# A two-layer Mamba stack with a soft mixture of experts: the second output projection ahead of x_proj, silus one scan later, the next chunk's w sooner

## The chip, the cores and the metric

The kernel runs on one core of one Trainium2 chip. The metric is the device time of one execution in microseconds (us). Everything is float32. The engines are named as in the profile: PE (matmuls and transposes; PEld loads its weights), DVE (vector), ACT (activations and copies), POOL (GpSimd), SP (issues DMAs).

## The reference

The input is 8192 rows of 512 numbers. Two Mamba layers are followed by a soft mixture of experts. Nearly all the time goes to the Mamba layers, and the change touches nothing else. One layer computes

```python
xz = x @ W_in.T;  xc, z = split(xz)              # 1024 channels each
u = silu(causal_conv4(xc) + b_c)
dt, Bm, Cm = split(u @ W_x.T)                    # 32, 16, 16 columns
delta = softplus(dt @ W_dt.T + b_dt)
h[t] = exp(delta * A) * h[t-1] + delta * u * Bm  # 16 states per channel
y = ((h * Cm).sum(states) + u * D) * silu(z)
out = y @ W_out.T
```

## The kernel before, in words

**Chunks, scans, slots.** Each layer works in 16 chunks of 512 rows: 32 chunks, numbered 0 to 31, in one unbroken stream over both layers. A chunk has 128 slots; two slots make a *scan step*, so a chunk has scan steps 0 to 63. Four scan steps do one half of the pairs (16 states, 2 halves of the channels), two blocks of 128 channels at a time.

**What each engine does in scan step p.**

- POOL (`inputs`, L1172) makes `bu`, the product of `w = delta * u` and the row of B. `bu` has three buffers, so the one for scan p can start when scan p-3 has ended.
- ACT (`head` L938, `decay_of` L928) copies the first elements of `bu` and makes two `decay` tiles. These have four buffers, two per scan, so the decays for scan p can start when scan p-2 has ended. Then it does what the timetable gives to the two slots: it *takes* finished tiles of PE out of PSUM, scales every fourth turned state (`product`, L958), and runs the silus and the softplus.
- DVE (`scan`, L1289) runs the scan over `decay` and `bu` into `h`, and then the multiply-adds (`add_state`, L1319, L1317) of the two turned states of the two slots. Where ACT takes both of them, which is in every scan step p = 2 modulo 4, DVE has no multiply-add.
- PE turns the states (128x128 transposes, L666) into two PSUM banks (`turn`), which alternate; a bank is free again when DVE or ACT has used it. Between the turns it runs the projections of the timetable, a few matmuls a slot, into two other banks (`proj`, `RING = 2`). Projection tile n waits until tile n-2 has been taken by ACT.

**The order.** Every engine runs its own list in order. `ORDER` (L41) is the order of the projection tiles of a chunk; `timetable` (L112 on) spreads their matmuls over the slots by weights and sets the slot in which ACT takes each tile: three slots after its last matmul, changed by `TAKE_LATER`. `conv_half` and `conv` are the input projection and the convolution of the next chunk, `x_proj`, `turn_c`, `delta_next` its x_proj, the turned C and the first half of its delta; `delta` is the second half of the present chunk's; `out` 0 to 3 is the output projection of the chunk before; `gate` 0 to 7 is z; `norm` 0 to 3 (chunks 0 to 13 alone) transposes the normalised rows of the chunk two later.

**The silus.** `silu_u` (L829) runs once per half over a 128x2048 tile, `silu_z` (L871) likewise. Each lies between two loads of ACT's function table. `SILU_LATER` (L54) gives how many slots after the last take of its half each silu stands. The matmuls of x_proj need both `silu_u`; the earliest slot of x_proj is worked out from `SILU_LATER[1]` too (L126).

**The w of the next chunk.** Between its `bu`, POOL adds up the softplus (`sum_delta`, L1154) and multiplies by u (`product`, L1161), in the scan steps that `W_AT` (L58) gives; `HEAD_AT` (L61) places the small operations that make the first elements of the next chunk (L1181 to L1200). Two more of POOL's jobs, the sums of products (L1214, L1223), lie at fixed places (`SUM_AT`).

**x_proj out of PSUM.** ACT's take of x_proj (L837 to L843) copies the tile, issues two DMAs and only then frees the bank. `turn_c` needs the copied tile.

Of the kernel before, what the change touches and what calls it, by code (L numbers as in the profile page):

```python
# [40 lines left out]
ORDER = [('conv_half', 0, 0), ('conv_half', 1, 0), ('delta', 4, 0), ('conv', 0, 8), ('conv_half', 2, 0), ('delta',  # L41
         5, 0), ('conv', 1, 0), ('conv_half', 3, 0), ('delta', 6, 0), ('conv', 2, 0), ('delta', 7, 0), ('conv_half',
         4, 0), ('conv', 3, 0), ('conv_half', 5, 0), ('conv', 4, 0), ('conv_half', 6, 0), ('conv', 5, 0),
         ('conv_half', 7, 0), ('conv', 6, 0), ('conv', 7, 0), ('norm', 0, 0), ('out', 0, 0), ('norm', 1, 8), ('norm', 2, 0),
         ('x_proj', 0, 0), ('norm', 3, 0), ('turn_c', 0, 0), ('out', 1, 0), ('delta_next', 0, 0),
         ('delta_next', 1, 0), ('out', 2, 0), ('delta_next', 2, 0), ('delta_next', 3, 4), ('out', 3, 0), ('gate', 0,
         4), ('gate', 1, 0), ('gate', 2, 0), ('gate', 3, 0), ('gate', 4, 0), ('gate', 5, 0), ('gate', 6, 0),
         ('gate', 7, 0)]
# [1 line left out]
SLOTS_BODY = GROUPS * HB  # L50
PAIRS = SLOTS_BODY // 2
TAKE_LAG, TAPS_LEAD, XDBL_LAG, CONV_LAG, PROD_LAG = 3, 2, 3, 3, 2
TAKE_LATER = {('out', 0): -1, ('gate', 0): 1, ('gate', 2): 2, ('delta_next', 0): -1, ('conv', 5): -1, ('delta', 5): -1}
SILU_LATER = (4, 4, 1, 1)  # L54
V_SUM_AT = (10, 10, 10, 10, 10, 10, 10, 9, 9, 9, 10, 10, 10, 10, 10, 9)
JOIN_AT = (41, 72)

W_AT = {13: ('sum', 2), 16: ('product', 2), 20: ('sum', 3), 23: ('product', 3), 47: ('sum_next', 0), 51:  # L58
        ('product_next', 0), 55: ('sum_next', 1), 59: ('product_next', 1)}

HEAD_AT = {24: ('exponent', 1), 28: ('state', 1), 56: ('exponent_next', 0), 61: ('state_next', 0)}  # L61
HEAD_EXP_AT = {51: ('exp', 1), 117: ('exp_next', 0)}
BFIRST_AT = 24

# [51 lines left out]
def timetable():  # L116
# [5 lines left out]
    for i, (kind, x, earliest) in enumerate(ORDER):  # L122
        if kind == "conv":
            earliest = max(earliest, end_of["conv_half", x] + CONV_LAG + TAKE_LATER.get(("conv_half", x), 0))
        if kind == "x_proj":
            earliest = end_of["conv", NB - 1] + TAKE_LATER.get(("conv", NB - 1), 0) + TAKE_LAG + SILU_LATER[1] + 4  # L126
        if kind in ("turn_c", "delta_next"):
            earliest = end_of["x_proj", 0] + XDBL_LAG + TAKE_LATER.get(("x_proj", 0), 0)
        slots = []
# [9 lines left out]
        end = end_of[kind, x] = slots[-1]  # L139
        late = end + TAKE_LAG + TAKE_LATER.get((kind, x), 0)  # L140
        if kind == "conv_half":
# [5 lines left out]
        if kind == "conv" and x % HB == HB - 1:  # L147
            take[late + SILU_LATER[x // HB]].append(("silu_u", x // HB, i))
        if kind == "gate" and x % HB == HB - 1:
            take[late + SILU_LATER[2 + x // HB]].append(("silu_z", x // HB, i))  # L150
    return work, take, end_of
# [142 lines left out]
def mamba_stack(nc, ctx, d, rstd, nmr):  # L294
# [828 lines left out]
    def _(pool):  # L1123
# [17 lines left out]
        def bias(X):  # L1141

            pool.wait_ge(norm_step, X * 11 + 11)
            rows = slice(X * J, X * J + J)
            pool.tensor_tensor(nmr[:, rows], neg_mean[:], rstd[:, rows], ALU.mult).then_inc(bias_set, 1)
# [91 lines left out]
        def body(G, kind):  # L1237
            for p in range(PAIRS):
                what, pair = W_AT.get(p, ("", 0))
                if what and kind.has(what.replace("sum", "delta").replace("product", "delta")):  # L1240
                    delta_w(G, what, pair)
                if p == BIAS_AT and kind.norms:
                    bias(G + NORM_AHEAD)
                if p in HEAD_AT:
                    what, hf = HEAD_AT[p]
                    X = G + what.endswith("_next")
# [906 lines left out]
```

## Time and profile before

| | us |
|---|---|
| median of 3 runs (7781.32 to 7786.65) | 7782.45 |
| the profiled execution's own time | 7782.23 |
| its span (first to last instruction) | 7780.4 |
| chunks 2 to 30, first scan to first scan of the next | 221.2 to 224.0 each |
| stretch before the first scan | 99.2 |
| stretch behind the last scan (mixture of experts) | 580.6 |
| DVE busy, share of the span | 7073.6, 91% |
| PE busy, share of the span | 7040.2, 90% |
| POOL busy, share of the span | 6668.8, 86% |
| ACT busy, share of the span | 6030.5, 78% |

The page lists what each engine was busy with and what ended its idle time. The trace behind it gives each instruction with its start (from the span's start), its duration and, in square brackets, the idle time of its engine before it and what ended that. All chunks of one kind repeat to a tenth of a microsecond, so one chunk can stand for many: chunk 20 (4541.3 to 4763.1) for the chunks without `norm`, chunk 8 (1875.9 to 2098.4) for those with it.

### The profile page before, as it was taken

Reading aid. Unit: us, or ns where it says so; the run is one execution under the profiler, and the core shown is the slowest. Engines: PE = TensorE matmul, PEld = TensorE weight load, DVE = VectorE, ACT = ScalarE, POOL = GpSimd, SP = SyncE. Lnnn points to the kernel's source line nnn. Section 1 sums busy time; section 2 is a strip of 40 time slices with the busy share of each in tenths; the row PEclk is TensorE's granted clock in tenths of the full one; section 3 lists DMA queues with packets and bytes.
Section 4 is the critical chain, followed back from the end, with each engine's and each line's share of the span. In section 5 each row is a group of like instructions: output and inputs, shape, how many; then the busy total and the mean of one; then the engine's idle time right before and its main releaser. Section 6 shows DMA issues by size and latency. Waiting matters only on the chain. (4 is left out here: it accounts for less than half of the span.)

```text
span 7780.4 us, 98947 instructions
## 1 busy us (share of the span) xinstructions
PE 7040.2 (90%) x29580; PEld 3887.5 (50%) x29580; DVE 7073.6 (91%) x6228; ACT 6030.5 (78%) x13267; POOL 6668.8 (86%) x3115
## 2 busy tenths in 40 slices
PE   7899999999999999999999999999999999987799
PEld 3454554554454545544444445444444454444664
DVE  5999999999999999999999999999999999999655
ACT  7888888888878888877777788777777787776564
POOL 5999999999999999999999999999999999998010
PEclk9899999999999999999999999999999999998899
DMA  3222222222222222222222222222222222221665
GB/s 107 76 85 86 79 86 77 79 76 82 86 85 79 86 77 79 77 84 87 85 69 75 66 75 70 75 71 75 68 74 66 75 70 76 70 71 51 246 234 184
DMA packets 282695, 684.05 MB, mean 88 GB/s; under 512 B 37872, under 2 KB 38128, under 8 KB 254384
## 3 DMA queue, kind: packets, MB, share of 16 engines
q1 hardware_dynamic: 252464, 626.31, 24.7%
q10 hardware_dynamic: 29696, 51.40, 1.8%
q8 instruction: 239, 3.92, 0.2%
q14 instruction: 296, 2.42, 0.1%
HBM read 508.76 MB, written 168.82 MB: 87 GB/s over the span
## 5 line engine op out<-in xcount | busy, mean ns | idle before, releaser
L1172 POOL TENSOR_TENSOR bu<-w,b_rep 128x1022 f32<-128x1022 f32 x2048 | 4802.0, 2363 | 489.6 <-DVE h L1289 483.1
L1289 DVE TENSOR_TENSOR_SCAN h<-decay,bu 128x1024 f32<-128x1024 f32 x2048 | 4651.4, 2282 | 213.3 <-ACT decay L928 109.2
L666 PEld LDWEIGHTS turn<-ident_m,h 128*128 128x128 f32 x16384 | 1974.0, 143 | 2687.0 <-issue 1297.0
L928 ACT ACTIVATE decay<-delta,neg_a 128x511 f32<-128x511 f32 x4096 | 2666.4, 685 | 714.1 <-DVE h L1289 711.2
L666 PE MATMUL turn<-ident_m,h 128*128 128x128 f32 x16384 | 2573.5, 282 | 503.5 <-DVE acc L1319 465.6
L1319 DVE SCALAR_TENSOR_TENSOR acc<-turn,c_now,acc 128x512 f32<-128x512 f32 x2816 | 1972.6, 738 | 126.6 <-PE turn L666 126.2
L958 ACT ACTIVATE prod<-turn,c_now 128x512 f32<-128x512 f32 x1024 | 700.5, 684 | 504.2 <-PE turn L666 487.0
L1214 POOL TENSOR_TENSOR prod<-prod 128x1024 f32<-128x1024 f32 x448 | 1059.9, 2366 | 10.0 <-ACT prod L958 10.0
L588 PE MATMUL proj<-x_conv,w_in 128*128 128x512 f32 x2048 | 1026.2, 598 | 45.3 <-ACT halo L818 36.1
L588 PE MATMUL proj<-conv_in,conv_diag 128*128 128x512 f32 x1984 | 989.8, 598 | 68.3 <-ACT halo L818 68.3
L588 PE MATMUL proj<-x_gate,w_in 128*128 128x512 f32 x2048 | 1016.9, 596 | 0.0
L588 PE MATMUL proj<-zy,w_out 128*128 128x512 f32 x1024 | 504.5, 595 | 0.0
L588 PE MATMUL proj<-w_out,zy 128*128 128x512 f32 x1024 | 503.6, 598 | 0.9 <-DVE zy L1328 0.9
L938 ACT COPY bu<-h_first 128x2 f32<-128x2 f32 x2048 | 385.4, 188 | 51.5 <-ACT stage L877 25.5
L588 PEld LDWEIGHTS proj<-conv_in,conv_diag 128*128 128x128 f32 x1984 | 316.2, 191 | 212.3 <-ACT halo L818 108.4
L588 PEld LDWEIGHTS proj<-x_conv,w_in 128*128 128x128 f32 x2048 | 327.5, 192 | 184.0 <-issue 106.5
L588 PEld LDWEIGHTS proj<-x_gate,w_in 128*128 128x128 f32 x2048 | 327.9, 192 | 113.6 <-issue 107.4
L1154 POOL TENSOR_TENSOR delta<-delta,w 128x1024 f32<-128x1024 f32 x128 | 303.1, 2368 | 41.2 <-ACT w L862 41.2
L808 ACT ACTIVATE conv_diag<-ident_m,par 128x128 f32<-128x128 f32 x992 | 315.2, 391 | 0.4
L588 PE MATMUL proj<-u,w_x 128*64 128x512 f32 x512 | 305.6, 707 | 10.2 <-ACT u L829 10.2
L1161 POOL TENSOR_TENSOR w<-delta,u 128x1024 f32<-128x1024 f32 x128 | 303.7, 2373 | 0.3
L1317 DVE TENSOR_SCALAR acc<-turn,c_now 128x512 f32<-128x512 f32 x256 | 189.3, 741 | 106.1 <-PE turn L666 104.0
(167 smaller groups left out, 5839.9 us busy)
## 6 DMA issues: line engine op xcount, KB each, us to landing
b_rep<-b_rows SPq DMA_DIRECT2D x1024, 256.0 KB, 3.3
u_rows<-u SPq DMA_DIRECT2D x64, 1024.0 KB, 4.0
u_back<-u_rows SPq DMA_DIRECT2D x256, 256.0 KB, 3.5
x_gate<-xt SPq DMA_DIRECT2D x32, 1024.0 KB, 7.0
xt<-stage ACTq DMA_DIRECT2D x128, 256.0 KB, 2.4
x_conv<-xt SPq DMA_DIRECT2D x31, 1024.0 KB, 6.3
x_gate<-in_x_dram SPq DMA_DIRECT2D x16, 1024.0 KB, 5.3
x_l<-in_x_dram SPq DMA_DIRECT2D x16, 1024.0 KB, 10.3
```

What stands on the lines that cost most here:

```text
L588: mm = pe.matmul(out[0:lhs.shape[1], :], lhs, rhs, start=n == 0, stop=n == count - 1)
L666: mm = pe.transpose(out[:, b * P:(b + 1) * P], h[:, (G * GROUPS + k) % H_RING, b, j * P:(j + 1) * P], ident[:])
L808: act.activation(conv_diag[:, b % 2, k, :], ident[:], ACT.Copy, scale=par[:, STATES + k, b:b + 1])
L928: act.activation(decay[:, (G * SLOTS_BODY + s) % DEC_RING, 1:T], delta[:, blk, 1:T], ACT.Exp, scale=neg_a[:, n, blk:blk + 1]).then_inc(dec ...
L938: act.copy(bu[:, (G * PAIRS + p) % BU_RING, :, 0], h_first[:, hf, n, 2 * pr:2 * pr + 2]).then_inc(head_set, 1)
L958: act.activation(prod[:, V_BUFFER[q], k % 2, :], turn[:, BANK[tile], :], ACT.Copy, scale=c_now[:, j, n:n + 1]).then_inc(v_done, 1)
L1154: pool.tensor_tensor(delta[:, lo:lo + 2, :], delta[:, lo:lo + 2, :], w[:, lo:lo + 2, :], ALU.add).then_inc(delta_set, 1)
L1161: pool.tensor_tensor(w[:, lo:lo + 2, :], delta[:, lo:lo + 2, :], u[:, lo:lo + 2, :], ALU.mult).then_inc(w_set, 2)
L1172: pool.tensor_tensor(bu[:, (G * PAIRS + s // 2) % BU_RING, :, 1:T], w[:, blk:blk + 2, 1:T], b_rep[:, g % B_RING, 1:T].unsqueeze(1).to_broa ...
L1214: pool.tensor_tensor(total, total, prod[:, V_BUFFER[q]], ALU.add).then_inc(vsum_set, 1)
L1289: dve.tensor_tensor_scan(h[:, (G * GROUPS + k) % H_RING, 2 * pr:2 * pr + 2, :].rearrange("p b t -> p (b t)"), decay[:, at:at + 2, :].rearr ...
L1319: dve.scalar_tensor_tensor(out, src, scalar, out, ALU.mult, ALU.add).then_inc(x_done, 1)
```

## The change

Four tables are changed; no instruction is added or removed, and DVE's order stays as it is.

```diff
-         ('conv_half', 7, 0), ('conv', 6, 0), ('conv', 7, 0), ('norm', 0, 0), ('out', 0, 0), ('norm', 1, 8), ('norm', 2, 0),
-         ('x_proj', 0, 0), ('norm', 3, 0), ('turn_c', 0, 0), ('out', 1, 0), ('delta_next', 0, 0),
+         ('conv_half', 7, 0), ('conv', 6, 0), ('conv', 7, 0), ('norm', 0, 0), ('out', 0, 0), ('norm', 1, 8),
+         ('out', 1, 0), ('x_proj', 0, 0), ('norm', 2, 0), ('norm', 3, 0), ('turn_c', 0, 0), ('delta_next', 0, 0),
...
-TAKE_LATER = {('out', 0): -1, ('gate', 0): 1, ('gate', 2): 2, ('delta_next', 0): -1, ('conv', 5): -1, ('delta', 5): -1}
-SILU_LATER = (4, 4, 1, 1)
+TAKE_LATER = {('out', 0): -1, ('gate', 0): 1, ('gate', 2): 2, ('turn_c', 0): -1, ('conv', 5): -1, ('delta', 5): -1}
+SILU_LATER = (6, 6, 4, 4)
...
-W_AT = {13: ('sum', 2), 16: ('product', 2), 20: ('sum', 3), 23: ('product', 3), 47: ('sum_next', 0), 51:
-        ('product_next', 0), 55: ('sum_next', 1), 59: ('product_next', 1)}
-
-HEAD_AT = {24: ('exponent', 1), 28: ('state', 1), 56: ('exponent_next', 0), 61: ('state_next', 0)}
+W_AT = {13: ('sum', 2), 16: ('product', 2), 20: ('sum', 3), 23: ('product', 3), 46: ('sum_next', 0), 49:
+        ('product_next', 0), 52: ('sum_next', 1), 56: ('product_next', 1)}
+
+HEAD_AT = {24: ('exponent', 1), 28: ('state', 1), 54: ('exponent_next', 0), 60: ('state_next', 0)}
```

What the timetable makes of it, in scan steps of a chunk:

| | before | changed |
|---|---|---|
| `silu_u` first half (ACT) | 20 | 21 |
| take of `out` 0 (ACT) | 32 | 32 |
| `silu_u` second half (ACT) | 32 | 33 |
| `out` 1 matmuls (PE) | 38 to 40 | 32 to 35 |
| x_proj matmuls (PE) | 34 to 36 | 35 to 38 |
| `norm` 2 and 3 transposes (PE) | 32 and 37 | 38 and 38 |
| take of x_proj (ACT) | 38 | 40 |
| `turn_c`, `delta_next` 0 and 1 (PE) | 38, 41, 41 | 40, 40, 40 |
| `silu_z` first half (ACT) | 56 | 57 |
| `silu_z` second half (ACT) | 1 of the next chunk | the same |
| last `gate` take (ACT) | 0 of the next chunk | 63 |

**ACT, chunks without `norm`, around the second half of `silu_u`** (scan steps 31 to 34). `decay` are the tiles for the scan, `stage` is the take of `out` 0, `prod` scaled turned states. Before:

```order
L958 ACTIVATE prod<-turn,c_now 128x512 x2
L938 COPY bu<-h_first 128x2
L928 ACTIVATE decay<-delta,neg_a 128x511 x2
L969 COPY h_last<-h 128x4
L829 ACT_TABLE_LOAD
L829 ACTIVATE u<-u 128x2048
L772 ACT_TABLE_LOAD
L877 COPY stage<-proj 128x512
L879 DMA xt<-stage 128x512
L938 COPY bu<-h_first 128x2
L928 ACTIVATE decay<-delta,neg_a 128x511 x2
```

Now:

```order
L958 ACTIVATE prod<-turn,c_now 128x512 x2
L938 COPY bu<-h_first 128x2
L928 ACTIVATE decay<-delta,neg_a 128x511 x2
L969 COPY h_last<-h 128x4
L877 COPY stage<-proj 128x512
L879 DMA xt<-stage 128x512
L938 COPY bu<-h_first 128x2
L928 ACTIVATE decay<-delta,neg_a 128x511 x2
L829 ACT_TABLE_LOAD
L829 ACTIVATE u<-u 128x2048
L772 ACT_TABLE_LOAD
L938 COPY bu<-h_first 128x2
```

The silu with its two loads has moved behind the decays of scan 33, and the take of `out` 0 stands ahead of those decays.

**PE, chunks with `norm`, the middle of the chunk** (scan steps 32 to 38). `u,w_x` is x_proj, `zy,w_out` is `out`, `ident_m,x_gate` is `norm`, `ident_m,h` the turned states. Before:

```order
L588 MATMUL proj<-zy,w_out 128x512 x2
L666 MATMUL turn<-ident_m,h 128x128 x4
L694 MATMUL proj<-ident_m,x_gate 128x128 x8
L666 MATMUL turn<-ident_m,h 128x128 x16
L588 MATMUL proj<-u,w_x 64x512 x2
L666 MATMUL turn<-ident_m,h 128x128 x4
L588 MATMUL proj<-u,w_x 64x512
```

Now, first ahead of x_proj and then behind its last matmul:

```order
L588 MATMUL proj<-zy,w_out 128x512 x2
L666 MATMUL turn<-ident_m,h 128x128 x4
L694 MATMUL proj<-ident_m,x_gate 128x128 x4
L588 MATMUL proj<-zy,w_out 128x512
L666 MATMUL turn<-ident_m,h 128x128 x4
L588 MATMUL proj<-zy,w_out 128x512
L666 MATMUL turn<-ident_m,h 128x128 x4
```

```order
L588 MATMUL proj<-u,w_x 64x512
L694 MATMUL proj<-ident_m,x_gate 128x128 x8
L666 MATMUL turn<-ident_m,h 128x128 x12
L634 MATMUL proj<-ident_m,xdbl 128x128 x4
L641 MATMUL proj<-xdbl,w_dt 128x512
L666 MATMUL turn<-ident_m,h 128x128 x4
L641 MATMUL proj<-xdbl,w_dt 128x512
```

The run of turned states without a projection between them (x16 before) is filled with `out` 1, and `norm` 2 and 3 stand together right behind x_proj. In chunks without `norm` the rows are the same without the L694 ones.

**POOL, the last third of a chunk** (scan steps 46 to 59). `delta` and `w` are the sums and products of the next chunk. Before:

```order
L1154 TENSOR_TENSOR delta<-delta,w 128x1024
L1172 TENSOR_TENSOR bu<-w,b_rep 128x2x511 x4
L1214 TENSOR_TENSOR prod<-prod 128x1024
L1161 TENSOR_TENSOR w<-delta,u 128x1024
L1172 TENSOR_TENSOR bu<-w,b_rep 128x2x511 x4
L1214 TENSOR_TENSOR prod<-prod 128x1024
L1154 TENSOR_TENSOR delta<-delta,w 128x1024
L1172 TENSOR_TENSOR bu<-w,b_rep 128x2x511
L1181 TENSOR_TENSOR a_first<-neg_a,delta 128x64
L1172 TENSOR_TENSOR bu<-w,b_rep 128x2x511 x3
L1214 TENSOR_TENSOR prod<-prod 128x1024
L1161 TENSOR_TENSOR w<-delta,u 128x1024
```

Now:

```order
L1154 TENSOR_TENSOR delta<-delta,w 128x1024
L1172 TENSOR_TENSOR bu<-w,b_rep 128x2x511 x3
L1161 TENSOR_TENSOR w<-delta,u 128x1024
L1172 TENSOR_TENSOR bu<-w,b_rep 128x2x511 x2
L1214 TENSOR_TENSOR prod<-prod 128x1024
L1172 TENSOR_TENSOR bu<-w,b_rep 128x2x511
L1154 TENSOR_TENSOR delta<-delta,w 128x1024
L1172 TENSOR_TENSOR bu<-w,b_rep 128x2x511 x2
L1181 TENSOR_TENSOR a_first<-neg_a,delta 128x64
L1172 TENSOR_TENSOR bu<-w,b_rep 128x2x511
L1214 TENSOR_TENSOR prod<-prod 128x1024
L1172 TENSOR_TENSOR bu<-w,b_rep 128x2x511
```

The same operations stand between the same `bu`, the last product (L1161) now three `bu` sooner.

## Rows read from the trace of the kernel before

**Rows 1.** The page, part 1: busy time (share of the span) and instructions of each engine.
```profile
PE 7040.2 (90%) x29580; PEld 3887.5 (50%) x29580; DVE 7073.6 (91%) x6228; ACT 6030.5 (78%) x13267; POOL 6668.8 (86%) x3115
```

**Rows 2.** Busy time by stretch: stretch, length, busy of PE, PEld, DVE, ACT, POOL, clock.
```profile
4541.00:4763.00 222.00, 203.74 (x856) 109.83 (x855) 209.54 (x169) 174.64 (x384) 207.01 (x97) 0.98 0.22 72
4657.00:4662.00 5.00, 3.90 (x8) 1.47 (x8) 5.00 (x5) 1.99 (x3) 3.38 (x2) 0.50 0.16 35
```

**Rows 3.** Timeline of DVE, chunk 20: start, us, what, [idle before, releaser].
```profile
4609.46 2.28 DVE L1289 TENSOR_TENSOR_SCAN h<-decay,bu 128x1024 f32<-128x1024 f32 x1
...
4614.24 2.29 DVE L1289 TENSOR_TENSOR_SCAN h<-decay,bu 128x1024 f32<-128x1024 f32 x1 [1.19 <-ACT decay L928]
...
4649.36 2.29 DVE L1289 TENSOR_TENSOR_SCAN h<-decay,bu 128x1024 f32<-128x1024 f32 x1
...
4655.11 2.29 DVE L1289 TENSOR_TENSOR_SCAN h<-decay,bu 128x1024 f32<-128x1024 f32 x1 [2.15 <-ACT decay L928]
...
4665.46 0.75 DVE L1317 TENSOR_SCALAR acc<-turn,c_now 128x512 f32<-128x512 f32 x1 [2.38 <-PE turn L666]
...
4667.72 2.28 DVE L1289 TENSOR_TENSOR_SCAN h<-decay,bu 128x1024 f32<-128x1024 f32 x1
...
4671.08 0.75 DVE L1317 TENSOR_SCALAR acc<-turn,c_now 128x512 f32<-128x512 f32 x1 [0.44 <-PE turn L666]
...
4680.61 0.75 DVE L1319 SCALAR_TENSOR_TENSOR acc<-turn,c_now,acc 128x512 f32<-128x512 f32 x1 [0.26 <-PE turn L666]
...
4730.26 2.29 DVE L1289 TENSOR_TENSOR_SCAN h<-decay,bu 128x1024 f32<-128x1024 f32 x1 [1.09 <-POOL bu L1172]
...
4738.29 2.29 DVE L1289 TENSOR_TENSOR_SCAN h<-decay,bu 128x1024 f32<-128x1024 f32 x1 [0.94 <-ACT decay L928]
```

**Rows 4.** Timeline of ACT, chunk 20, at the two `silu_u`.
```profile
4607.47 1.28 ACT L829 ACT_TABLE_LOAD   x1
4608.76 1.91 ACT L829 ACTIVATE u<-u 128x2048 f32<-128x2048 f32 x1
4610.69 1.28 ACT L772 ACT_TABLE_LOAD   x1
...
4652.65 0.59 ACT L877 COPY stage<-proj 128x512 f32<-128x512 f32 x1
...
4653.63 0.19 ACT L938 COPY bu<-h_first 128x2 f32<-128x2 f32 x1 [0.40 <-ACT stage L877]
4653.73 1.29 ACT L928 ACTIVATE decay<-delta,neg_a 128x511 f32<-128x511 f32 x2
```

**Rows 5.** Timeline of PE, chunk 20, scan steps 32 to 36.
```profile
4648.42 1.88 PE L588 MATMUL proj<-w_out,zy 128*128 128x512 f32 x4
...
4658.10 1.11 PE L666 MATMUL turn<-ident_m,h 128*128 128x128 f32 x4 [4.43 <-DVE acc L1319]
4659.14 3.68 PE L588 MATMUL proj<-u,w_x 128*64 128x512 f32 x4
```

**Rows 6.** Timeline of POOL, chunk 20, from the `bu` of scan 45 on.
```profile
4690.64 2.36 POOL L1172 TENSOR_TENSOR bu<-w,b_rep 128x1022 f32<-128x1022 f32 x1 [1.08 <-DVE h L1289]
...
4741.86 4.72 POOL L1172 TENSOR_TENSOR bu<-w,b_rep 128x1022 f32<-128x1022 f32 x2
```

**Rows 7.** Timeline of PE, chunk 8, end of `out` 0 and `norm` 1.
```profile
1984.86 1.88 PE L588 MATMUL proj<-zy,w_out 128*128 128x512 f32 x4
...
1987.02 0.60 PE L694 MATMUL proj<-ident_m,x_gate 128*128 128x128 f32 x4
```

**Rows 8.** Timeline of ACT, chunk 8, the take of x_proj.
```profile
2007.47 0.58 ACT L837 COPY xdbl<-proj 64x512 f32<-64x512 f32 x1 [0.63 <-PE proj L588]
...
2008.91 0.16 ACT L843 COPY spare_m<-proj 128x1 f32<-128x1 f32 x1 [0.87 <-ACT xdbl L837]
```

**Rows 9.** Timeline of DVE, chunk 8: scans 32 and 36.
```profile
1985.73 2.28 DVE L1289 TENSOR_TENSOR_SCAN h<-decay,bu 128x1024 f32<-128x1024 f32 x1
...
2003.10 2.28 DVE L1289 TENSOR_TENSOR_SCAN h<-decay,bu 128x1024 f32<-128x1024 f32 x1
```

## The prediction

> **What bounds the kernel now.** I read the page first: DVE and PE are busy 91% and 90% of the span, POOL 86% [rows 1]. Over one chunk DVE works 209.5 of 222 us, POOL 207.0, PE 203.7 [rows 2]. So no engine can save more than its idle 12.5 us in a chunk, and since DVE's own list is unchanged, the question is where those 12.5 us lie. DVE's timeline says it [rows 3]: it never drifts, it stops at a few fixed places. In chunk 20 these are scan 21 (1.19 us, waits for the decay), scan 33 (2.15, the decay), the multiply-adds behind scan 35 (2.38, waits for PE), those behind 36 and 39 (0.44, 0.26), scan 55 (1.09, waits for POOL) and scan 57 (0.94, the decay). The chain of waits on the page covers only the tail and tells nothing of this. About 0.2% of 7782, or 16 us, is what a measurement here can tell from no change.
>
> The pace between stops, from the same timeline: a scan takes 2.2 us of DVE's time and two multiply-adds 1.3, so a step is 3.5 us, or 2.2 where ACT takes both states (p = 2 modulo 4).
>
> **Silus, the rule.** A silu holds ACT for 1.28 + 1.91 + 1.28, 4.50 us with the hand-overs [rows 4]. The decays for scan p may start at the end of scan p-2 and take 1.39 us with the head copy (4653.63 to 4655.02 [rows 4]). With the silu behind them, the next decays end 1.39 + 4.50 + 1.39 = 7.3 us after that start, plus ACT's other work; DVE needs them three sets of multiply-adds and two scans later: 8.3 us if all three have two, 7.0 if one is empty. Steps 20, 32 and 56 have an empty one; 21, 33 and 57 do not. This is what the move buys.
>
> **Scan 21.** The take of `conv_half` 5 (three copies, 4611.97 on) now goes ahead of them, in free time. The decays of 21 start at the end of scan 19 (4609.46 less 1.3 of multiply-adds, 4608.2) and end at 4609.65, the silu ends at 4614.2, the take of `conv` 4 (0.7) at 4614.9, the decays of 22 at 4616.25. Scan 22 is due at 4609.46 + 7.0 = 4616.46 [rows 3]. The 1.19 go. But ACT's scaled states two steps on come late against the faster DVE, and PE may not turn the second state of step 23 before its bank is free; following that chain (turn 0.45, matmul 0.87, turn, matmul, turn) gives back 0.7. **Gain 0.5 per chunk**; bounds 0 and 1.2. All 31 chunks.
>
> **Scans 33 to 39 without `norm`** (chunks 14 to 30, 17 of them). ACT now takes `out` 0 ahead of the decays of 33. PE ends `out` 0 at 4650.30 [rows 5], so ACT, done with the decays of 32 by then, waits; its copy and DMA issue cost 0.98 (4652.65 to 4653.63 [rows 4]); the decays of 33 end at 4652.7, just in time for 4649.36 + 3.5 = 4652.86 [rows 3]. The silu ends at 4657.3, the decays of 34 at 4658.75, but scan 34 is due at 4656.36: a stop of 2.5, one scan later than the old 2.15. So the silu itself gains nothing here. What goes is what came behind it. Before, PE has nothing but turns between `out` 0 and x_proj, stands 4.43 us, and then runs the first two x_proj matmuls in 3.68 us [rows 5]. The granted clock there is 0.50, the lower level of 1.2 GHz [rows 2]; at 2.4 GHz they would need half. That is why the adds behind 35 wait 2.38. Now `out` 1 fills the hole: PE turns and multiplies in pairs of 1.3 us, two pairs a step against 3.5, and stands at most 1.4 us. Scan 34 starts at 4658.85, 35 at 4661.05, 36 at 4664.55, where the trace has 4667.72 [rows 3]: 3.2 us. The x_proj pairs (1.6 us each, 3.2 per step) fit under DVE's 3.5, so 0.44 and 0.26 go too. **Gain 3.9**; bounds 0 (the clock falls all the same) and 5.
>
> **The same place with `norm`** (chunks 0 to 13, 14 of them). `out` 0 ends at 1986.74 and `norm` 1 stands between [rows 7]; `out` 1's first matmul delays the next turn to 1988.9 where the add is due at 1988.58 (1985.73 + 2.85 [rows 9]): 0.35. The decays of 33 end at 1989.2, the silu at 1993.8, the take of `norm` 1 (0.98) at 1994.8, the decays of 34 at 1996.2, scan 36 starts at 2002.0 against 2003.10 [rows 9]: 1.1 better. Then the two PSUM banks bite. `norm` 3 stands on PE two tiles behind x_proj and waits until ACT has freed x_proj's bank; ACT takes x_proj only behind the decays of 40, after scan 38 (2011.2), and frees the bank 1.6 us after it begins (2007.47 to 2009.07, with two DMA issues [rows 8]): at 2015.0. All turns queue behind `norm` 3 on PE, so the add behind scan 39, due at 2013.4, gets its state at 2016.1: a stop of 2.7. **Loss 0.7 by scan 40** in place of a gain; bounds a gain of 2.5 (no such stop) and a loss of 3.
>
> **x_proj, turn_c, delta_next (scans 40, 41).** PE: turned C at 136.0 us of the chunk, `delta_next` 0 to 137.4, `delta_next` 1 when ACT has taken the turned C (137.6, behind the decays of 41), `out` 2 when ACT has taken `delta_next` 0 (138.7), the next turned state at 140.2, needed at 141.7. 1.5 to spare: nothing. SP's queue keeps its order; b_rows is stored two scan steps later, and its reader is the next chunk's.
>
> **The w of the next chunk.** From scan 45 on POOL does not wait for anyone until the `bu` of 59: it starts at 4690.64 and starts that one at 4741.86 [rows 6]. In between lie the same operations as before, so its end cannot move. Before, w is last of them and the stops are at 51, 55 and, hidden under POOL, at 57. Now POOL's work comes at 52 and 56, so DVE meets it at 51, 52, 55 and 56; by 2.3 us per POOL operation the `bu` of 56 is ready at 4735.1, and 3.5 + 3.5 + 2.8 later scan 59 starts at 4745.0, 0.4 after today's. The 0.94 at scan 57 vanish under it. **Loss 0.4 per chunk**; bounds 0 and 1.2.
>
> **Sum.** 17 x (0.5 + 3.9 - 0.4) = 68; 14 x (0.5 - 0.7 - 0.4) = -8.4; chunk 31 has no silu_u and no next w, so only its silu_z: 0.9. Together 60.5. From the profiled 7782.2 (span 7780.4 and 1.8 around it; the median of the runs is 7782.45, the same) that is **7721.5 us**.
>
> **A rule against it.** The loads of the function table stand at 1.28 us, with the silu 0.01 behind the first one [rows 4]. The Trainium skill's page "ScalarE: Activation LUTs", section "What ACT_TABLE_LOAD costs", adds a drain of about 1.38 us to each, 2.66 in all. By that page's figure, as an estimate, a silu would hold ACT 2.8 us longer than the trace shows. The trace disagrees, and the sum goes by the trace.
>
> **Rivals.**
> - *The two banks cost nothing with `norm`* (0.15): if ACT reaches x_proj while scan 39 runs, the 2.7 of 14 chunks go: 7721.5 - 38 = 7683.5. For it: the whole list of ACT there is light. Against: the take stands behind decays that cannot start before scan 38 ends.
> - *PE still falls to the lower clock* (0.10): the stop of 2.5 at scan 34 leaves PE without banks as before. Then the stops behind 35 and later stay, and 33 to 39 lose 0.3 instead of gaining 3.9: 7721.5 + 17 x 4.2 = 7793. Against: PE's hole was 4.43 long, and seven matmuls now stand in it.
> - *A new serial chain at scans 40 and 41* (0.08), slower: x_proj, turned C, `delta_next` 0, `delta_next` 1 and `out` 2 hand two banks to and fro with ACT, which takes each only behind decays. I find 1.5 us to spare; if two of the takes come a full step (3.5) later each, 5.5 are lost in 31 chunks, 170 in all: 7891. It cancels the gain from 2.0 us per chunk on.
> - *The loads grow when a decay waits behind them* (0.01), the rule above as a mechanism: if each took twice its row, 2.6 more per silu, less the 0.2 and 1.0 spare at 22 and 58, would stop DVE 2.4 + 2.6 + 1.6 us in 31 chunks: 7721.5 + 205 = 7926.
> - The w part does nothing or little by my own working; that rival is in the forecast.
>
> **How the numbers follow.** Forecast 0.66, rivals 0.15, 0.10, 0.08, 0.01. With its bounds (0.5 us either way in 31 chunks, 1 in 17, 2 in 14, not all at once) the forecast spans some 7685 to 7765. The range 7672 to 7778 holds nearly all of that, most of the first rival and the better part of what lies between forecast and second. Faster by over 0.2%: the forecast, the first rival and a little of the second, 0.83; within 0.2%: 0.09; slower: 0.08.
>
> **What would show it.** Right: no stop at scans 21 and 57; scan 34 waits about 2.5 for the decay; no stretch at clock 0.5 in chunks 14 to 30 and no wait for PE behind 35; chunks 14 to 30 at about 217.8 us, chunks 2 to 13 still near 223, with a wait of over 2 us for PE behind scan 39; stops for POOL at 51, 52 and 56. Wrong: half clock still there, waits at 41 to 43, or equal gains with and without `norm`.

## The result and the profile after

The changed kernel takes 7704.86 us (median of 4 runs, 7704.26 to 7708.81) against 7783.26 us of the kernel before, run beside it: 78.4 us less, ratio 0.990, 95% interval 0.9883 to 0.9917. The forecast was 7721.5 us, 17 us too high.

The profiled execution took 7704.26 us, its span is 7702.5. Busy time by engine, the row that answers to [rows 1]:

```profile
PE 7011.1 (91%) x29580; PEld 3860.8 (50%) x29580; DVE 7066.7 (92%) x6228; ACT 6029.3 (78%) x13267; POOL 6663.3 (87%) x3115
```

The work is the same; PE needs 29 us less for the same matmuls. The lower of the two clocks (granted share 0.50) was in force for 272 us of the span, where it had been for 410. The length of the stages, from the first scan of a chunk to that of the next, read off DVE's timeline of both traces, in us:

| stage | before | after | forecast of the gain | gain |
|---|---|---|---|---|
| up to the first scan | 99.2 | 100.4 | 0 | -1.2 |
| chunks 0 to 13 (with `norm`), sum | 3112.1 | 3114.8 | -8.4 | -2.7 |
| chunks 1 to 13, median of one | 222.63 | 222.24 | | |
| chunks 14 to 30, sum | 3770.2 | 3695.4 | 68 | 74.8 |
| chunks 14 to 30, median of one | 221.82 | 217.19 | | |
| chunk 31 | 218.24 | 212.07 | 0.9 | 6.2 |
| the rest | 580.6 | 579.7 | 0 | 0.9 |

**Chunk 20**, which lasted 222.0 us before. The stretches, as in [rows 2]; the second is the middle of the chunk, where the clock stood at 0.50 before:

```profile
4520.00:4737.20 217.20, 201.52 (x853) 108.16 (x853) 209.00 (x170) 174.29 (x384) 206.57 (x97) 1.00 0.23 73
4630.00:4645.00 15.00, 13.44 (x53) 6.28 (x53) 12.72 (x11) 12.85 (x24) 11.66 (x6) 1.00 0.42 136
```

DVE's idle time in the chunk has gone from 12.5 to 8.2 us. Its stops over 0.4 us, from the timeline of DVE, to be laid beside [rows 3]:

```profile
4546.40 0.75 DVE L1319 SCALAR_TENSOR_TENSOR acc<-turn,c_now,acc 128x512 f32<-128x512 f32 x1 [0.75 <-PE turn L666]
4560.88 0.75 DVE L1319 SCALAR_TENSOR_TENSOR acc<-turn,c_now,acc 128x512 f32<-128x512 f32 x1 [0.98 <-PE turn L666]
4601.32 0.75 DVE L1319 SCALAR_TENSOR_TENSOR acc<-turn,c_now,acc 128x512 f32<-128x512 f32 x1 [0.46 <-PE turn L666]
4636.69 4.47 DVE L1289 TENSOR_TENSOR_SCAN h<-decay,bu 128x1024 f32<-128x1024 f32 x2 [2.28 <-PE turn L666]
4690.13 2.29 DVE L1289 TENSOR_TENSOR_SCAN h<-decay,bu 128x1024 f32<-128x1024 f32 x1 [0.45 <-POOL bu L1172]
4694.75 2.29 DVE L1289 TENSOR_TENSOR_SCAN h<-decay,bu 128x1024 f32<-128x1024 f32 x1 [1.03 <-PE turn L666]
4708.92 2.29 DVE L1289 TENSOR_TENSOR_SCAN h<-decay,bu 128x1024 f32<-128x1024 f32 x1 [1.02 <-ACT decay L928]
```

They stand behind scans 7 and 11 (as before), behind scan 23, at scan 34, and at 51, 52 and 56. The stops at 21, 33 and 57, and those behind 35, 36 and 39, are gone. The releaser named for scan 34 was long done; what came last is in ACT's timeline:

```profile
4628.30 0.58 ACT L877 COPY stage<-proj 128x512 f32<-128x512 f32 x1 [2.23 <-PE proj L588]
...
4629.38 1.29 ACT L928 ACTIVATE decay<-delta,neg_a 128x511 f32<-128x511 f32 x2
4630.69 1.28 ACT L829 ACT_TABLE_LOAD   x1
4631.98 1.92 ACT L829 ACTIVATE u<-u 128x2048 f32<-128x2048 f32 x1
4633.92 1.28 ACT L772 ACT_TABLE_LOAD   x1
...
4635.31 1.29 ACT L928 ACTIVATE decay<-delta,neg_a 128x511 f32<-128x511 f32 x2
```

ACT waits 2.23 us for `out` 0, then come decays 33, the silu and decays 34, which end at 4636.60, and scan 34 starts at 4636.69. PE at the same place, where [rows 5] had the hole of 4.43 and four x_proj matmuls in 3.68 us:

```profile
4638.68 0.66 PE L666 MATMUL turn<-ident_m,h 128*128 128x128 f32 x4 [1.20 <-ACT prod L958]
...
4640.56 1.93 PE L588 MATMUL proj<-u,w_x 128*64 128x512 f32 x4
```

From scan 32 to 38 the longest hole is 1.20 us, and four x_proj matmuls take 1.93 us.

In the middle the clock stays up in all of chunks 14 to 30, but not everywhere in them: it falls during scan 63 of chunks 17, 20, 25 and 29, which no chunk's length shows, and at scan 4 of chunks 15 and 27. These last 218.6 and 218.9 us, since DVE waits 2.04 us behind scan 4 where chunk 20 has 0.35. In chunk 15, the clock and DVE:

```profile
3446.70:3450.00 3.30, 3.30 (x5) 1.13 (x5) 1.86 (x2) 3.30 (x9) 3.30 (x3) 0.50 0.33 111
```

```profile
3450.61 0.75 DVE L1317 TENSOR_SCALAR acc<-turn,c_now 128x512 f32<-128x512 f32 x1 [2.04 <-PE turn L666]
```

So one chunk does not always stand for all of its kind.

**Chunk 8**, with `norm`. DVE at scan 34 and behind 39, then PE behind x_proj:

```profile
1997.17 4.47 DVE L1289 TENSOR_TENSOR_SCAN h<-decay,bu 128x1024 f32<-128x1024 f32 x2 [2.88 <-ACT decay L928]
2016.39 1.41 DVE L1319 SCALAR_TENSOR_TENSOR acc<-turn,c_now,acc 128x512 f32<-128x512 f32 x2 [2.08 <-PE turn L666]
```

```profile
2012.51 0.66 PE L694 MATMUL proj<-ident_m,x_gate 128*128 128x128 f32 x4
2015.26 0.66 PE L694 MATMUL proj<-ident_m,x_gate 128*128 128x128 f32 x4 [2.10 <-ACT spare_m L843]
...
2018.96 1.92 PE L641 MATMUL proj<-xdbl,w_dt 65*128 65x512 f32 x2
```

`norm` 3 waits 2.10 us until ACT has freed x_proj's bank (L843 is its last read), and all turned states wait behind it. In this chunk the granted clock falls to half from 2016.5 on, so that the next two matmuls take 1.92 us and DVE waits 1.12, 1.32 and 0.97 us more: the chunk lasts 225.9 us. In chunk 9 the clock falls at the same place for a shorter time: DVE waits 2.47 us behind scan 39, and the chunk lasts 222.8 us. Chunks 1 to 7 and 10 to 13 have the same hole of 2.10 us and keep the clock behind it.

### The profile page after: what moved, and what is told of

The parts are those of the page before. It is cut to its first block and busy times, and to the rows that moved or that the text cites. A ratio compares the mean times of both kernels' runs of the same rounds, so it can differ in the third digit from the quotient of the medians.

```text
span 7702.5 us, 98947 instructions
## 1 busy us (share of the span) xinstructions
PE 7011.1 (91%) x29580; PEld 3860.8 (50%) x29580; DVE 7066.7 (92%) x6228; ACT 6029.3 (78%) x13267; POOL 6663.3 (87%) x3115
## 5 line engine op out<-in xcount | busy, mean ns | idle before, releaser
L1161 POOL TENSOR_TENSOR w<-delta,u 128x1024 f32<-128x1024 f32 x128 | 303.4, 2370 | 0.3
L674 PE MATMUL turn<-u_back,d_diag 128*128 128x512 f32 x512 | 283.3, 635 | 2.5 <-DMA u_back<-u_rows 1.2
L588 PE MATMUL proj<-u,w_x 128*64 128x512 f32 x512 | 270.9, 623 | 10.2 <-ACT u L829 10.2
```

The source lines that it names most:

```text
L588: mm = pe.matmul(out[0:lhs.shape[1], :], lhs, rhs, start=n == 0, stop=n == count - 1)
L1161: pool.tensor_tensor(w[:, lo:lo + 2, :], delta[:, lo:lo + 2, :], u[:, lo:lo + 2, :], ALU.mult).then_inc(w_set, 2)
```

## The experiments

All times are medians of runs beside the kernel before on the same chip; it took 7783.78 us beside the first four, 7785.47 beside the next four and 7782.73 beside the last three. "P" in an expectation is the prediction's own account, "S" its rival.

### One part alone

**The order of projections alone**, the silus left at their places:

```diff
-TAKE_LATER = {('out', 0): -1, ('gate', 0): 1, ('gate', 2): 2, ('delta_next', 0): -1, ('conv', 5): -1, ('delta', 5): -1}
-SILU_LATER = (4, 4, 1, 1)
+TAKE_LATER = {('out', 0): -1, ('gate', 0): 1, ('gate', 2): 2, ('turn_c', 0): -1, ('conv', 5): -1, ('delta', 5): -1}
+SILU_LATER = (4, 4, 3, 4)
```
with the changed kernel's ORDER.

> The kernel before with the new order of tiles alone (out 1 ahead of x_proj, norm 2 and 3 behind it); all silus stay in the scan steps they had. Theory P (out 1 fills PE's hole and the clock stays up): chunks 14 to 30 fall from 221.8 to about 217.7 us although the silu still stops DVE by about 2.1 us at scan 33, since the waits for PE behind scans 35, 36 and 39 go; no half clock there; chunks 1 to 13 near 223, chunk 31 some 5 us shorter; total about 7710 us. Theory S (the gain of the change comes from where the silus stand): no more than 10 us off the 7783 of before, and the waits behind 35 stay because they follow from the silu's stop.

Measured: 7734.41 us, ratio 0.9939 (0.9926 to 0.9951). That is slower than the 7710 of the first account and far from the second. Chunks 14 to 30 have a median of 219.37 us, 1 to 13 of 223.43, chunk 31 takes 213.01. PE in chunk 20, and the clock there:

```profile
4651.25 0.66 PE L666 MATMUL turn<-ident_m,h 128*128 128x128 f32 x4 [2.61 <-DVE acc L1319]
4651.75 2.78 PE L588 MATMUL proj<-w_out,zy 128*128 128x512 f32 x4
```

```profile
4651.00:4656.00 5.00, 4.75 (x13) 2.64 (x14) 5.00 (x4) 2.15 (x4) 3.92 (x2) 0.66 0.05 16
```

`out` 1 doesn't close the hole by itself: DVE still stops 2.15 us at scan 33, PE runs out of states to turn, stands 2.61 us, and here comes back at the lower clock. But chunk 20 is one of 8 in the profiled execution (7740.10 us) where it does: 15, 16, 17, 20, 21, 23, 24 and 29. In the other 9 of chunks 14 to 30 the hole is the same 2.61 us and the clock stays up, as in chunk 18:

```profile
4213.73 0.65 PE L666 MATMUL turn<-ident_m,h 128*128 128x128 f32 x4 [2.61 <-DVE acc L1319]
4214.23 1.88 PE L588 MATMUL proj<-w_out,zy 128*128 128x512 f32 x4
```

From scan 32 to scan 40 these 9 take 28.05 us, the 8 take 29.45 to 29.75; the kernel before takes 31.91. So where the clock stays up, the order alone gains 3.9 us in the middle of the chunk, and the fall of the clock takes 1.4 to 1.7 of it back.

**The silus alone**, the order of projections untouched (the `+ 2` keeps x_proj where it was):

```diff
-SILU_LATER = (4, 4, 1, 1)
+SILU_LATER = (6, 6, 2, 1)
-            earliest = end_of["conv", NB - 1] + TAKE_LATER.get(("conv", NB - 1), 0) + TAKE_LAG + SILU_LATER[1] + 4
+            earliest = end_of["conv", NB - 1] + TAKE_LATER.get(("conv", NB - 1), 0) + TAKE_LAG + SILU_LATER[1] + 2
```

> The kernel before with the silus alone one scan step later (21, 33, 57); x_proj's matmuls stay in the slots they had, the order of tiles too. Theory P: scan 21's stop of 1.19 us goes and 0.5 come back behind scan 23, 0.6 to 0.7 us per chunk or 20 us in all; in the middle PE still has its hole, waits for the silu one scan longer and runs x_proj at half clock, so 33 to 39 get no better or up to 2 us worse per chunk: total between 7760 and 7800 us. Theory S: at least 50 us off, 7733 or less.

Measured: 7715.89 us, ratio 0.9914 (0.99 to 0.9927): the rival's number. Chunks 14 to 30 have a median of 218.66, 1 to 13 of 221.84. PE in chunk 20:

```profile
4624.30 1.32 PE L666 MATMUL turn<-ident_m,h 128*128 128x128 f32 x8 [1.18 <-DVE acc L1319]
4627.80 0.66 PE L666 MATMUL turn<-ident_m,h 128*128 128x128 f32 x4 [2.18 <-DVE acc L1319]
4628.39 1.93 PE L588 MATMUL proj<-u,w_x 128*64 128x512 f32 x4
```

With the decays of scan 33 ahead of the silu, DVE goes on through scan 33 and its adds, so PE has states to turn in the middle of its hole: 1.18 and 2.18 us in place of 4.43. In chunk 20 x_proj then runs at full clock (the clock falls there later, at scan 37, as it does in chunk 24). In the other 15 of the 17 chunks it still halves at this place, as in chunk 19:

```profile
4407.50:4411.30 3.80, 2.20 (x6) 1.24 (x7) 2.20 (x3) 3.77 (x5) 3.45 (x2) 0.50 0.36 149
```

but x_proj starts at 4410.14, while DVE stands until 4411.98 for the decays of scan 34. Its first four matmuls take 3.68 us, 1.75 more than in chunk 20, and DVE waits only 0.80 us behind scan 35, where it had waited 2.38 and 0.84 us.

**The w part alone** (W_AT and HEAD_AT of the change, in the kernel before), and **the change without it** (the old W_AT and HEAD_AT in the changed kernel):

```diff
-W_AT = {13: ('sum', 2), 16: ('product', 2), 20: ('sum', 3), 23: ('product', 3), 47: ('sum_next', 0), 51:
-        ('product_next', 0), 55: ('sum_next', 1), 59: ('product_next', 1)}
-HEAD_AT = {24: ('exponent', 1), 28: ('state', 1), 56: ('exponent_next', 0), 61: ('state_next', 0)}
+W_AT = {13: ('sum', 2), 16: ('product', 2), 20: ('sum', 3), 23: ('product', 3), 46: ('sum_next', 0), 49:
+        ('product_next', 0), 52: ('sum_next', 1), 56: ('product_next', 1)}
+HEAD_AT = {24: ('exponent', 1), 28: ('state', 1), 54: ('exponent_next', 0), 60: ('state_next', 0)}
```

> The kernel before with the new places of the next chunk's w and first elements alone. Theory P: POOL does not wait from the bu of scan 45 to that of 59, so the order in between can only move the stops: stops for POOL at 51, 52, 55 and 56 in place of 51, 55 and the silu's at 57, and 0.3 to 0.4 us more per chunk, 10 us in all: 7793 us. Rival: the w was late for the next chunk, and sooner gains 0.5 us or more per chunk: 7768 us or less.

> The changed kernel with the next chunk's w and first elements back where they were. Theory P: stops for POOL at 51 and 55 alone, 0.3 us less per chunk than the changed kernel, 7695 us against its 7705. Rival (w sooner is what makes room for the later silu_z): 7705 or more, with a stop at scan 57 or 58.

Measured: 7798.71 us for the part alone, ratio 1.0021 (1.0012 to 1.003), and 7689.06 us without it, ratio 0.9878 (0.9864 to 0.9891), 15.8 us under the changed kernel. The stops of chunk 20 without it are one less and 0.4 us shorter in sum (0.45, 1.09 and 0.84 at scans 51, 55 and 59, against 0.45, 1.03, 0.27 and 1.02 at 51, 52, 55 and 56):

```profile
4678.76 2.29 DVE L1289 TENSOR_TENSOR_SCAN h<-decay,bu 128x1024 f32<-128x1024 f32 x1 [0.45 <-POOL bu L1172]
4692.63 2.29 DVE L1289 TENSOR_TENSOR_SCAN h<-decay,bu 128x1024 f32<-128x1024 f32 x1 [1.09 <-POOL bu L1172]
4706.84 2.29 DVE L1289 TENSOR_TENSOR_SCAN h<-decay,bu 128x1024 f32<-128x1024 f32 x1 [0.84 <-ACT bu L938]
```

The part costs time in either kernel. In the changed one it is 0.47 us in a chunk with `norm` and 0.40 in one without (medians of 222.24 and 217.19 us against 221.77 and 216.79). In the kernel before it is 0.93 us (medians of 222.63 and 223.56) and 0.08 (221.82 and 221.90): there the stops from scan 51 on grow by about 1 us too, but in chunk 20 the wait behind scan 35 is 1.46 us in place of 2.38. Behind the same hole of 4.4 us the clock comes back sooner there: the first four x_proj matmuls take 3.18 us in place of 3.68, the turned states behind them 0.66 in place of 1.08.

### The clock alone

Five idle matmuls in PE's hole, in the kernel before:

```diff
+                if s == 67 and not kind.norms and not kind.last:
+                    spare = bank(G, kind, ORDER.index(("x_proj", 0, 0)))
+                    for _ in range(FILL):
+                        pe.matmul(spare, ident[:], w_out[:, 0, :], start=True, stop=True)
```

> The kernel before with five idle matmuls (128 columns by 512, into x_proj's own bank ahead of its first real matmul, so the result is untouched) in TensorE's hole of 4.43 us of chunks 14 to 30. Nothing else moves. Theory of the clock: the granted clock no longer halves behind the hole, the waits for TensorE behind scans 35, 36 and 39 (3.2 us with the stop at 33 apart) shrink to 0.5 us or less, 17 x 2.7 = 46 us less: about 7738 us. Rival, from the run with the silus moved alone (which kept the halved clock and was 68 us faster): the halved clock costs little by itself, the lateness of the adds and of x_proj does: 7775 to 7785 us.

Measured: 7743.12 us, ratio 0.9946 (0.9932 to 0.9959). Chunks 14 to 30 have a median of 219.22 against 221.82 us, the others stay. PE, and the clock:

```profile
4643.15 4.46 PE L729 MATMUL proj<-w_out,ident_m 128*128 128x512 f32 x10
...
4648.34 1.93 PE L589 MATMUL proj<-u,w_x 128*64 128x512 f32 x4
```

```profile
4647.00:4652.00 5.00, 4.86 (x18) 1.71 (x17) 5.00 (x5) 3.09 (x6) 3.73 (x2) 1.00 0.11 23
```

In the trace of this kernel the granted clock never falls in chunks 14 to 30; before, it did in each of the 17. DVE still stops 2.16 us at scan 33 but waits only 0.69 behind 35, where it waited 2.38 and 0.84. So 2.6 us of a chunk hang on the clock, with nothing else moved but the filled hole. The run with the silus alone had the lower clock in most chunks and was faster still: lateness and clock are two prices of one hole, and either repair takes most of both.

### What is left at scans 34 and 39

**`out` 0 taken behind the silu** in the chunks without `norm` (the change without its w part, the take moved from slot 65 to 67):

```diff
+        if (kind, x) == ("out", 0):
+            take[late + 2].append(("out_behind", x, i))
...
+                if what == "out" and x == 0 and not kind.norms or what == "out_behind" and kind.norms:
+                    continue
+                what = "out" if what == "out_behind" else what
```

> e4_after_w_back, in which ScalarE takes output 0 of the second projection behind silu_u's half and not ahead of it, in the chunks without norm. Cause tested: VectorE's stop of 2.28 us at scan 34, in chunks 14 to 30, is made by the order take of output 0 (for which ScalarE waits 2.23 us in chunk 20), decays, silu. If the wait for output 0 makes it, the stop falls to 0.2 to 0.3 us and the chunks from 216.8 to 214.6 us: 7689 less 17 x 2.1 = 7653 us. Rival: the silu with its two table loads (4.5 us) makes the stop whatever stands ahead of it: the chunks stay at 216.8 and the time at 7685 to 7692 us. Second rival: the later take only moves the stop to scan 36 (x_proj waits for the bank): above 7692 us.

Measured: 7653.39 us, ratio 0.9831 (0.9817 to 0.9844). Chunks 14 to 30: 214.82 us. ACT in chunk 20 (lines stand two further on in this kernel):

```profile
4600.44 1.30 ACT L930 ACTIVATE decay<-delta,neg_a 128x511 f32<-128x511 f32 x2
4601.76 1.28 ACT L831 ACT_TABLE_LOAD   x1
4603.05 1.92 ACT L831 ACTIVATE u<-u 128x2048 f32<-128x2048 f32 x1
4604.99 1.28 ACT L774 ACT_TABLE_LOAD   x1
4606.29 0.58 ACT L879 COPY stage<-proj 128x512 f32<-128x512 f32 x1
```

No wait for `out` 0 stands ahead of the silu, and the stop at scan 34 is gone (0.22 us are left, behind 36). The silu of 4.5 us fits; the wait of 2.23 us for `out` 0 did not.

**Norms ahead**, one place each (like all that follow, without the w part):

```diff
-         ('conv_half', 7, 0), ('conv', 6, 0), ('conv', 7, 0), ('norm', 0, 0), ('out', 0, 0), ('norm', 1, 8),
-         ('out', 1, 0), ('x_proj', 0, 0), ('norm', 2, 0), ('norm', 3, 0), ('turn_c', 0, 0), ('delta_next', 0, 0),
+         ('conv_half', 7, 0), ('conv', 6, 0), ('conv', 7, 0), ('norm', 0, 0), ('norm', 1, 8), ('out', 0, 0),
+         ('norm', 2, 0), ('out', 1, 0), ('x_proj', 0, 0), ('norm', 3, 0), ('turn_c', 0, 0), ('delta_next', 0, 0),
```

> e4_after_w_back with norm 1 ahead of output 0, norm 2 ahead of output 1 and both ahead of x_proj in the order of PSUM takes. Cause tested: the stop of 2.2 us behind scan 39 in chunks 0 to 13 comes from norm 3 waiting for x_proj's bank. If it does, behind x_proj norm 3 needs only output 1's bank, the stop goes, and chunks 0 to 13 fall by 2.0 to 2.3 us each: 7689 less 30 = 7659 us; chunks 14 to 30 unchanged at 216.8. Rival: the wait is of the work on TensorE at that place, not of the bank, and comes back at another scan of 34 to 41: 7680 to 7695 us.

Measured: 7641.06 us, ratio 0.9815 (0.9801 to 0.9828), and that for another reason than the one given. Chunks 1 to 13 did not gain (median 221.73, without the edit 221.77), chunks 14 to 30 did: 214.51. PE and ACT in chunk 8:

```profile
1980.23 1.54 PE L588 MATMUL proj<-zy,w_out 128*128 128x512 f32 x2 [2.59 <-ACT stage L877]
...
1982.42 2.78 PE L588 MATMUL proj<-zy,w_out 128*128 128x512 f32 x4
```

```profile
1978.30 1.28 ACT L772 ACT_TABLE_LOAD   x1
1979.60 0.58 ACT L877 COPY stage<-proj 128x512 f32<-128x512 f32 x1
```

The stop behind 39 went, as expected. In its place `out` 1 needs the bank of `out` 0, whose copy now stands behind the silu: PE stands 2.59 us, comes back at the lower clock, and DVE waits 1.57 and 2.26 us behind scan 33.

**The two together**:

> Both edits, the take of output 0 behind the silu in chunks without norm and the norms' banks ahead of x_proj's in those with norm. They touch different chunks, so if both causes stand the gains add: 7689 less 36 less 30 = 7623 us. If one falls the sum loses its part (7653 or 7659 us); if both fall 7689 us.

Measured: 7644.10 us, ratio 0.9817 (0.9803 to 0.983), no less than the norms alone. The gains don't add, since the second edit holds the first: in the kernel with the norms alone, ACT's timeline has the copy of `out` 0 behind the silu in chunk 20 too:

```profile
4594.09 1.28 ACT L772 ACT_TABLE_LOAD   x1
4595.39 0.59 ACT L877 COPY stage<-proj 128x512 f32<-128x512 f32 x1
```

A `norm` that the chunk doesn't have still takes its room in the timetable, so `out` 0 ends a place later, and its take with it. The next run puts just the take back.

```diff
-TAKE_LATER = {('out', 0): -1, ('gate', 0): 1, ('gate', 2): 2, ('turn_c', 0): -1, ('conv', 5): -1, ('delta', 5): -1}
+TAKE_LATER = {('out', 0): -2, ('gate', 0): 1, ('gate', 2): 2, ('turn_c', 0): -1, ('conv', 5): -1, ('delta', 5): -1}
```

> e6_norms_ahead with output 0 taken one slot sooner, that is ahead of the silu again; nothing else. e6 was 48 us under e4 where 30 were expected, and all of it in chunks 14 to 30, which I had not meant to touch: there a norm that does not exist still moved output 0 by a place in the timetable, and its take behind the silu. If that is the whole of it, chunks 14 to 30 go back to 216.8 (3690 us in all) and the time to 7680 to 7690 us; in chunks 0 to 13 the 3.8 us behind scan 33 turn into a stop of about 2.9 at scan 34. Rival: the order of the norms themselves gained there: 7641 us stays.

Measured: 7686.64 us, ratio 0.9874 (0.9861 to 0.9888). Chunks 14 to 30 are back at 217.18 us, chunks 1 to 13 stay at 221.82, with 3.32 us (chunk 8) at scan 34 in place of the waits behind 33. In chunk 20 the stop is this:

```profile
4616.80 4.47 DVE L1289 TENSOR_TENSOR_SCAN h<-decay,bu 128x1024 f32<-128x1024 f32 x2 [2.34 <-ACT decay L928]
```

**Three norms ahead, and all four**, so that only x_proj needs the bank of `out` 0:

```diff
-         ('conv_half', 7, 0), ('conv', 6, 0), ('conv', 7, 0), ('norm', 0, 0), ('norm', 1, 8), ('out', 0, 0),
-         ('norm', 2, 0), ('out', 1, 0), ('x_proj', 0, 0), ('norm', 3, 0), ('turn_c', 0, 0), ('delta_next', 0, 0),
+         ('conv_half', 7, 0), ('conv', 6, 0), ('conv', 7, 0), ('norm', 0, 0), ('norm', 1, 8), ('norm', 2, 0),
+         ('out', 0, 0), ('out', 1, 0), ('x_proj', 0, 0), ('norm', 3, 0), ('turn_c', 0, 0), ('delta_next', 0, 0),
```

> e4_after_w_back with norms 0, 1 and 2 ahead of output 0, then outputs 0 and 1, x_proj, norm 3. Output 0's take falls behind the silu in all chunks, and here output 1 does not need output 0's bank (it has norm 2's), x_proj does. Theory: what stopped chunks 0 to 13 (2.92 us at scan 34, 2.2 behind 39; with the norms one place ahead 3.8 us behind scan 33) was a projection that needed, in the ring of two banks, the bank whose copy stood around the silu. Then both stops go, about 1 us is left for the norms' banks in a row ahead of output 0: chunks 0 to 13 fall from 221.8 to 217.5 to 218.5, 14 x 3.8 = 53 us below 7641: 7588, range 7580 to 7605. Rival: the three norms in a row stop TensorE for about as long at scans 28 to 31: 7625 to 7645 us.

> As the run before, with norm 3 too ahead of output 0. One more PSUM bank to be taken in a row at scan 29, and output 1 ends a slot later. Theory: a stop of 0.5 to 1 us more at scans 29 to 31, none behind x_proj: 7585 to 7605 us. Output 1 needs output 0's bank no more than in the run before? It does: with four norms ahead the banks go norm 0 A, 1 B, 2 A, 3 B, output 0 A, output 1 B, x_proj A, so still only x_proj waits for output 0's. Rival: norms in a row stop TensorE: above the run before by over 10 us.

Measured: 7591.35 us with three, ratio 0.9752 (0.9739 to 0.9765), the fastest kernel here; 7618.86 us with four, ratio 0.9789 (0.9775 to 0.9802). The first came out as expected (7588), the second did not (7585 to 7605): it is the rival's number, for a reason that neither account had. Chunks 1 to 13 have medians of 217.71 and 219.10 us. With four, PE and ACT in chunk 8:

```profile
1952.93 1.12 PE L588 MATMUL proj<-zy,w_out 128*128 128x512 f32 x2 [1.39 <-ACT conv_in L918]
```

```profile
1952.29 0.59 ACT L918 COPY conv_in<-proj 128x512 f32<-128x512 f32 x1 [1.47 <-DMA xt<-conv_in]
```

The copy of `norm` 2 waits 1.47 us for the DMA that empties its staging tile. That wait is there with three norms as well (1.46 us), but then `out` 0 follows in the bank of `norm` 1 and PE doesn't notice. With four, `out` 0 needs the bank of `norm` 2, PE stands 1.39 us, and DVE waits 0.94 and 0.55 behind scan 31. Against the order with one place each, two things differ in chunks with `norm`: in both orders the take of `out` 0 stands behind the silu, but only here does `out` 1 not need its bank. The three norms ahead with the take ahead of the silu were not run.

## Why the prediction was right, and where not

The time came out in the range, by the forecast's account for the most part, and 17.5 us better than its sum: 5.7 in chunks 0 to 13, 6.8 in 14 to 30, 5.3 in chunk 31, less 0.3 outside. That the sum came so near although one of its steps was wrong has a plain reason: both edits at the middle of the chunk are in the change, so it did not matter which of them got the credit.

- **Scan 21**: the stop went. The give-back was worked out at 0.7 and stands as 0.46 behind scan 23: the gain is 0.7 where 0.5 was said.
- **Scans 33 to 39 without `norm`**: said 3.9, measured 4.2 (scan 32 to scan 40 takes 27.72 us in place of 31.91, mean of chunks 18 to 29). Each step is in the trace: ACT's wait for `out` 0, decays 33 on time, the stop moved to 34 (2.5 said, 2.28 measured), PE's holes under 1.4 (1.20), clock at 1.00 there, no waits at 35, 36 and 39. The list of stops that the prediction began with leaves out 0.84 behind 35 as well as 0.74 behind 7, 0.98 behind 11 and 0.48 at 51 (which is named only later, under w); the first goes with its neighbour, the others stay.
- **"So the silu itself gains nothing here" failed.** The run with the silus alone gained 68 us with `out` 1 in its old place. The step counted the silu's move as a stop shifted by one scan and gave the whole end of the hole to `out` 1. But the adds of the scans that are now on time give PE turned states to make, and that breaks the hole as well. By single parts the gains are 49 and 68 us, together 95 (the change without w): they are two repairs of the same place. From scan 32 to 40 the silus alone take 29.37 us (mean of chunks 18 to 29), the order alone 28.05 where the clock stays up, both 27.72, where the kernel before takes 31.91. So the prediction's 3.9 for `out` 1 is right in 9 of 17 chunks, and there the silu adds 0.3. In the other 8 `out` 1 alone does not keep the clock up behind its hole of 2.61 us; with the silu moved too, it stays up in all 17.
- **With `norm`**: the stop behind 39 through the ring of two banks was said as 2.7 and is 2.1 in chunk 8, 2.15 on average, with the releaser that was named. From scan 32 to 40 a chunk loses 0.29 (mean of chunks 2 to 13), not 0.7. What was not said is the fall of the clock behind that stop, of chunks 1 to 13 in 8 and 9 alone.
- **w**: said a loss of 0.4 in a chunk, measured 0.40 and 0.47. The stops are those named: 51, 52, 55 and 56.
- **Chunk 31**: said 0.9, measured 6.2. The prediction counted only what the chunk lacks (no silu_u, no next w) and did not look at its own waits. The order alone brings 5.2 of it (218.24 to 213.01), the silus alone 1.8. The forecast's 0.9 is chunk 20's stop at scan 57, but chunk 31 has its own:

```profile
7116.10 0.75 DVE L1319 SCALAR_TENSOR_TENSOR acc<-turn,c_now,acc 128x512 f32<-128x512 f32 x1 [1.54 <-PE turn L666]
7176.29 2.29 DVE L1289 TENSOR_TENSOR_SCAN h<-decay,bu 128x1024 f32<-128x1024 f32 x1 [2.01 <-ACT decay L928]
```

The second is scan 57; it goes to 0.29 (at 58) with the silus alone, to 0.98 with the order alone. The first is one of four waits for PE behind scans 39 and 43, 3.49 us together, which go with the order alone, as does one of 0.91 behind 14; with the silus alone they stay. In the changed kernel none of these is left.
- **The rivals**: the two banks did cost; the clock did not fall in the middle of chunks 14 to 30, which is what that rival was about, though the sign named for it, no stretch at 0.5 in these chunks, is not met: there are six, at scans 63 and 4; there is no wait at scans 40 and 41 in chunk 20. The table loads did not grow: 1.28 us each, the silu 0.01 us behind the first, with decays right behind them. The Trainium skill's page "ScalarE: Activation LUTs", section "What ACT_TABLE_LOAD costs", adds a drain to each; no row here shows it.

## What to carry to other kernels

When an in-order engine has a long piece of work to place (here a silu of 4.5 us), look at what the queue waits for just ahead of it: here a wait of 2.23 us cost 1.97 of each chunk (216.79 to 214.82), and putting the take of `out` 0 behind the silu was worth 36 us, nearly half as much as the whole change. With a ring of two banks, go through the takes in order and ask for each tile which copy it waits for, and where that copy stands; three small tiles ahead of the big ones changed the pairs, and together with the later take they brought chunks 1 to 13 from 221.77 to 217.71 us, while the later take with the wrong pairs gained nothing there (221.73). Look at many chunks before calling one typical: chunk 20 alone would say that the new order loses the clock, and it does so in 8 chunks of 17. Test parts alone before adding their gains: two edits may mend the same hole, or one may contain the other.

## What was not expected of the hardware

- The granted clock of PE halved behind holes a good deal shorter than the one of 4.43 us: 2.61 (order alone), 2.59 (norms ahead) and, in chunk 8 of the changed kernel, 2.10 us. It doesn't follow the hole alone: with the order alone the hole of 2.61 us is in all of chunks 14 to 30 and the clock falls behind it in 8; every chunk from 1 to 13 of the changed kernel has that hole of 2.10 us, and the clock falls behind it in chunks 8 and 9 only; and with the silus alone, where chunks 14 to 30 have holes of 1.18 and 2.18 us one after the other, it fell there in 15 of them, not in 20 and 24. Holes of 1.20 (changed kernel, chunks 14 to 30) and 1.39 us (four norms ahead, chunk 8) were followed by matmuls at full clock. What decides between chunks with the same holes is open.
- Filling the hole with idle matmuls is worth 42 us of 7785 by itself: work that computes nothing made the kernel faster.
